# Attention of a decoder layer: the rows transposed by the host, key tiles added on GpSimd, and projections and sums moved between the scores

## The reference

```python
x = x + attn(layernorm(x))                       # 16 query heads, 4 key/value heads, 32 wide
#   Q = rmsnorm(xn @ Wq); V = xn @ Wv; K = rmsnorm(V)      (K is made from V)
#   p = softmax(Q K^T)       (the mask is empty: all 256 x 256 scores count)
#   y = rmsnorm((p V) @ Wo)
x = x + xattn(ctx, ctx, layernorm(x))            # long convolution, by Toeplitz matrices
x = x + ffn(layernorm(x))                        # ternary weights, int8 activations, 2048 wide
```

## Time and profile before

| | us |
|---|---|
| median of the three runs | 678.32 |
| profiled execution, device time | 679.29 |
| profiled execution, span of the core | 677.5 |
| TensorE busy | 613.7 |
| VectorE busy | 485.3 |
| ScalarE busy | 455.3 |
| GpSimd busy | 269.8 |

### The profile page before, as it was taken

The page is one execution under the profiler, slowest core; times in us unless marked ns, Lnnn a source line. Parts: engine busy times, 40 slices in busy tenths (PEclk is TensorE's granted clock), DMA queues, the critical chain, the costliest instruction groups (busy, mean ns, idle before and its releaser), DMA issues.

```text
span 677.5 us, 10465 instructions
## 1 busy us (share of the span) xinstructions
PE 613.7 (91%) x2818; PEld 342.0 (50%) x2818; DVE 485.3 (72%) x949; ACT 455.3 (67%) x799; POOL 269.8 (40%) x248
## 2 busy tenths in 40 slices
PE   5889999999999999989999999957799999899975
PEld 4525454535454543367777777743344444444432
DVE  3455767575758372437778877898999999999961
ACT  2363666666666667158988888864778778688771
POOL 1000000100010001137777777742566666666671
PEclk9959999999999997989999999987999999999997
DMA  8473144536261717026555656431042342432424
GB/s 312 126 207 85 40 105 145 122 126 138 110 176 71 208 41 178 24 79 193 169 169 171 192 170 174 156 110 44 16 109 63 82 105 62 106 79 62 94 48 108
DMA packets 75589, 80.89 MB, mean 119 GB/s; under 512 B 38000, under 2 KB 49776, under 8 KB 75440
## 3 DMA queue, kind: packets, MB, share of 16 engines
q1 hardware_dynamic: 75568, 80.65, 43.1%
HBM read 47.51 MB, written 4.28 MB: 76 GB/s over the span
## 4 chain that ended last, share of the span: by engine, by line
PE 26%; DVE 16%; issue 7%; POOL 3%; ACT 2%; DVEq 1%; DMA 1%; ACTq 0%; POOLq 0%; SPq 0%
PE ps L708 20%; DVE toep L1189 3%; PE ps L1069 3%; PE ps L1057 2%; DVE mb L1193 2%; POOL big L1306 2%; DVE ps L1175 1%; DVE ps L1156 1%; DVE mx L1160 1%; DVE qo L761 1%; POOL r L1302 1%; ACT asq L1104 1%; DMA act8t<-ys 1%; ACT kv L1093 1%; DVE x_all L1138 1%
## 5 line engine op out<-in xcount | busy, mean ns | idle before, releaser
L708 PE MATMUL ps<-kv,toep 128*128 128x288 f32 x640 | 157.3, 409 | 1.1 <-PEq L1368 1.1
L708 PEld LDWEIGHTS ps<-kv,toep 128*128 128x128 f32 x640 | 122.3, 192 | 36.1 <-issue 2.4
L1069 PE MATMUL ps<-wt,xqt 128*128 128x512 bf16 x512 | 123.4, 387 | 17.3 <-DVE toep L1189 16.5
L1306 POOL TENSOR_TENSOR big<-toep,wst 128x512 f32<-128x512 f32 x64 | 82.9, 1295 | 41.9 <-DVE toep L1189 41.9
L396 ACT ACTIVATE big<-ps,kscale 128x512 f32<-128x512 f32 x128 | 85.5, 696 | 12.7 <-PE ps L246 10.3
L1069 PEld LDWEIGHTS ps<-wt,xqt 128*128 128x128 bf16 x512 | 48.5, 99 | 79.1 <-DVE toep L1189 24.2
L246 PE MATMUL ps<-qx,kx 128*128 128x512 f32 x128 | 78.3, 633 | 10.5 <-ACT big L396 8.6
L761 DVE TENSOR_REDUCE qo<-big 128x2048 f32 (+1 forms) x32 | 72.2, 2258 | 0.0
L1057 PE MATMUL ps<-wt,act8t 128*128 128x512 bf16 x256 | 60.3, 390 | 7.9 <-DMA act8t<-ys 7.0
L696 POOL TENSOR_TENSOR kv<-ctx 128x768 f32<-128x768 f32 (+1 forms) x32 | 52.7, 1648 | 36.7 <-PE ps L708 27.9
L750 DVE TENSOR_TENSOR big<-ps,qd 128x1024 f32<-128x1024 f32 x32 | 39.2, 1224 | 37.1 <-ACT ys L840 34.6
(11 more groups left out here) (118 smaller groups left out, 958.9 us busy)
## 6 DMA issues: line engine op xcount, KB each, us to landing
qx<-kv SPq DMA_DIRECT2D x128, 128.0 KB, 2.4
wst<-in_wall SPq DMA_DIRECT2D x12, 1024.0 KB, 6.4
wst<-in_wall SPq DMA_DIRECT2D x48, 256.0 KB, 3.7
toep<-krows SPq DMA_DIRECT2D x32, 256.0 KB, 3.7
ctx<-in_ctxt SPq DMA_DIRECT2D x32, 192.0 KB, 2.6
out_y<-ot SPq DMA_DIRECT2D x16, 256.0 KB, 2.9
conv_part<-qo SPq DMA_DIRECT2D x14, 256.0 KB, 2.7
x_all<-in_x SPq DMA_DIRECT2D x2, 1536.0 KB, 14.5
```

The source lines that it names most:

```text
L708: mm = pe.matmul(m.ps[:, LB * r + lb, :].rearrange("p (b s) -> p b s", s=WIDE)[:, :, 0:PAIRS], m.toep[r][:, d * P:(d + 1) * P], m.kv[r][:, ...
L1069: mm = pe.matmul(bank[:, n % 2, :], xqt[r][:, k, :], wt[:, k, n * C:(n + 1) * C], start=(k == 0), stop=(k == CK - 1))
L1306: nc.gpsimd.tensor_tensor(act_w[r][:, n * C:(n + 1) * C], a[n % 2][:], gb[:, n * C:(n + 1) * C], ALU.mult).then_inc(s_w.sem, 1)
```

## The change

- The host also hands over x transposed (`xt`). Sync loads a row's 512 KB into a buffer (`xt_first`, `xt_s`: two parts of `qo`), one row ahead (`next_rows`), and the transposes, their copies and the normalisation ahead of them go. In their place the weights Wq and Wv are centred over their input channels once in the prologue (`column_sums`, `centre`), the inverse deviation cancels in the queries and keys (`ev1` enters the root), and the values are scaled by it on GpSimd (`values`).
- The order of scores becomes: all groups for the first half gp of the queries, then all for the second.
- GpSimd adds the two key tiles of the weights (`add_weights`), and `sum_weights` runs over the sums: 16 instructions a turn. Each half of `sum_weights` and `sum_values` has a place of its own among the last scores or behind them, and each half its own PSUM bank.
- v and q of row 1 move, but for half of q, from the prologue into turn 0.
- VectorE: residual of row i - 1 at the head of turn i; one sum of squares per position tile; the first reciprocal ahead of the second sum of squares, the norms and the queries' normalisation; the small tiles of the norms, but for `rqk`, lie in PSUM.
- ScalarE: the weight-magnitude sums behind the copies of queries and keys. Sync: the loads of the FFN's weights wait for the 7th score.

```diff
+    pts = sb("pts", [P, 6, C])
...
+    norms = TB[:, 1, :].rearrange("p (a t n) -> p a t n", t=TT, n=P // 2)
+    ssq, ve2, gr, nt = (norms[:, a, :, 0:NH] for a in range(4))
+    value_bank, weight_bank = (OB[:, 0, :], SB[:, 1, :]), (OB[:, 1, :], SB[:, 0, :])
...
     def score(n):
-        return n // 4, n // 2 % 2, n % 2
+        return n // 2 % HKV, n % 2, n // (2 * HKV)
...
+        def next_rows(i):
+            wait(sp, s_q, i, 2)
+            sp.dma_start(xt_s, xt[bass.ds(i + 1, 1)].rearrange("o p k t -> (o p) k t")).then_inc(d_xt.sem, 16)
...
-        sp.dma_start(x_all[:, 0], x_in[:, 0]).then_inc(d_x0.sem, 16)
         sp.dma_start(wv_s[:], wv.rearrange("(k p) n -> p k n", p=P)).then_inc(d_wv.sem, 16)
         sp.dma_start(wq_s[:], wq.rearrange("(k p) n -> p k n", p=P)).then_inc(d_wq.sem, 16)
+        sp.dma_start(xt_first, xt[0]).then_inc(d_xt0.sem, 16)
+        sp.dma_start(x_all[:, 0], x_in[:, 0]).then_inc(d_x0.sem, 16)
+        sp.dma_start(xt_s, xt[1]).then_inc(d_xt.sem, 16)
         sp.dma_start(x_all[:, 1], x_in[:, 1]).then_inc(d_x1.sem, 16)
...
+        next_rows(1)
         spread_q(1)
         with sp.Fori(2, B - 1) as i:
+            next_rows(i)
             spread_q(i)
+            wait(sp, s_sc, i, 7)
+            apart(sp)
...
         def qk_transpose(i, after=True):
...
             wait(pe, s_klo, i, 1)
+            q_rows(0)
+            wait(pe, s_qn, i, 2)
             for kv in range(HKV):
...
+            q_rows(1)
...
         def scores(i, n):
             kv, s, gp = score(n)
-            if n % 4 == 0:
+            if n < 2 * HKV and s == 0:
                 wait(pe, d_qx[kv], i, 4 * 16)
-            if n % 8 == 0:
-                wait(pe, s_kx, i, n // 8 + 1)
+            if n in (0, HKV):
+                wait(pe, s_kx, i, kv // 2 + 1)
             if n >= 2:
                 wait(pe, s_e, i, n - 1)
...
+        def sum_weights(i, gp, has_prev):
+            wait(pe, s_ps, i, HKV * (gp + 1))
+            if gp == 0 and has_prev:
+                wait(pe, s_x1, i - 1, 2)
+            for kv in range(HKV):
+                mm = pe.matmul(weight_bank[gp][kv * DH:(kv + 1) * DH, :], m.ones[:, 0:DH], pts[:, (gp * HKV + kv) % 6, :],
+                               start=True, stop=True)
+            mm.then_inc(s_den.sem, 1)
+
+        def sum_values(i, gp, s, has_prev):
+            if s == 0:
+                wait(pe, s_e, i, 2 * HKV * (gp + 1))
+            if s == 0 and gp == 0:
+                wait(pe, s_vo, i, 1)
+                if has_prev:
+                    wait(pe, s_x1, i - 1, 1)
+                else:
+                    wait(pe, s_qn, i + 1, 1)
+            for kv in range(HKV):
+                mm = pe.matmul(value_bank[gp][kv * DH:(kv + 1) * DH, :], vo[:, s, kv * DH:(kv + 1) * DH],
+                               pt[:, s, kv, gp * C:(gp + 1) * C], start=(s == 0), stop=(s == TT - 1))
+            if s == TT - 1:
                 mm.then_inc(s_pv.sem, 1)
         def project(i, first):
...
         def turn(i, has_prev=True, has_next=True):
-            makes_next = has_prev and has_next
             scores(i, 0)
             scores(i, 1)
             for t in range(TT):
-                if makes_next:
-                    x_transpose(i + 1, t)
+                if has_next:
+                    v(i + 1, t)
                 scores(i, 2 + t)
-            for t in range(TT):
-                if makes_next:
-                    v(i + 1, t)
-                scores(i, 4 + t)
             for n in range(TT * CK):
-                if makes_next:
+                if has_next and has_prev:
                     q(i + 1, n // CK, n % CK)
-                scores(i, 6 + n)
-            for t in range(TT):
-                scores(i, 14 + t)
-            sum_weights(i)
-            for t in range(TT):
-                if has_prev:
-                    q2_transpose(i - 1, t, has_next)
-            if not has_prev:
-                wait(pe, s_qn, i + 1, 2)
-            sum_values(i)
+                elif has_next and n < CK:
+                    q(i + 1, 1, n)
+                scores(i, 4 + n)
+                if n == 6:
+                    sum_weights(i, 0, has_prev)
+            scores(i, 12)
+            sum_values(i, 0, 0, has_prev)
+            scores(i, 13)
+            sum_values(i, 0, 1, has_prev)
+            scores(i, 14)
+            if has_prev:
+                q2_transpose(i - 1, 0, has_next)
+            scores(i, 15)
+            for s in range(TT):
+                sum_values(i, 1, s, has_prev)
+            sum_weights(i, 1, has_prev)
+            if has_prev:
+                q2_transpose(i - 1, 1, has_next)
...
+        pe.wait_ge(c_ones.sem, 1)
+        pe.wait_ge(d_wv.sem, 16)
+        column_sums(SB[:, 1, 0:P], wv_s, c_wvsum)
+        pe.wait_ge(c_wqadd.sem, 2)
+        column_sums(SB[:, 0, :], qn[:, 0:1, :], c_wqsum)
+        pe.wait_ge(d_xt0.sem, 16)
+        pe.wait_ge(c_wv.sem, 1)
+        for t in range(TT):
+            v(0, t, rows=xt_first)
+        for n in range(TT * CK):
+            if n < CK:
+                pe.wait_ge(c_wq.sem, n + 1)
+            q(0, n // CK, n % CK, rows=xt_first)
+
+        pe.wait_ge(d_xt.sem, 16)
+        for k in range(CK):
+            q(1, 0, k, bank=OB[:, 0, :])
...
+            for n in range(3):
+                exponential(i, n)
...
+                k_square(i + 1)
+            exponential(i, 3)
+            if has_next:
+                k_high(i + 1)
             exponential(i, 4)
+            if has_next:
+                v_copy(i + 1)
+            for n in range(5, 8):
                 exponential(i, n)
+            if has_next:
+                q_square(i + 1, 0 if has_prev else 1)
+            for n in range(8, 11):
                 exponential(i, n)
+            if has_next and has_prev:
                 q_square(i + 1, 1)
+            for n in range(11, 16):
                 exponential(i, n)
             for t in range(TT):
                 if has_prev:
                     q2_out(i - 1, t)
             if has_next:
-                if has_prev:
-                    weight_sums(i)
                 qk_out(i + 1)
+            if has_next and has_prev:
+                weight_sums(i)
             project(i, has_prev)
...
+        def rows_var(i, first=False):
+            if not first:
+                wait(dve, s_rs1, i - 1, 1)
             layer_norm_stats(i, stats, mv, ve1, s_bn1, s_mv1, s_ve1)
-            wait(dve, s_rs1, i, 1)
-            for t in range(TT):
-                if not first:
-                    wait(dve, s_xt, i - 1, t + 1)
-                nc.vector.tensor_scalar(xn[:, t, :], row(i, t), mv[:, t, 0:1], rs1[:, t:t + 1],
-                                        ALU.subtract, ALU.mult).then_inc(s_xn.sem, 1)
+            nc.vector.tensor_scalar(ev1[:], mv[:, :, 1], LN_EPS, RMS_EPS, ALU.add, ALU.mult).then_inc(s_ev1.sem, 1)
...
+        def qk_sums(i, t):
+            wait(dve, s_sq, i, t + 2)
+            nc.vector.tensor_reduce(ssq[:, t, :], sq[:, t, :].rearrange("p (n d) -> p n d", d=DH),
+                                    AX.X, ALU.add).then_inc(s_ssq.sem, 1)
+
         def qk_norms(i):
-            for part, (lo, hi) in enumerate(((0, NV + HQ), (NV + HQ, NH))):
-                wait(dve, s_sq, i, part + 2)
-                nc.vector.tensor_reduce(ssq[:, lo:hi], sq[:, lo * DH:hi * DH].rearrange("p (n d) -> p n d", d=DH),
-                                        AX.X, ALU.add).then_inc(s_ssq.sem, 1)
             wait(dve, s_ssq, i, 2)
-            nc.vector.tensor_scalar(ve2[:], ssq[:], 1.0 / DH, RMS_EPS, ALU.mult, ALU.add).then_inc(s_ve2.sem, 1)
+            wait(dve, s_ev1, i, 1)
+            nc.vector.scalar_tensor_tensor(ve2, ssq, 1.0 / DH, spread(ev1[:], NH), ALU.mult, ALU.add
+                                           ).then_inc(s_ve2.sem, 1)
...
+                nc.vector.tensor_tensor(gr, ve2, rqk[:], ALU.mult).then_inc(s_nr.sem, 1)
                 wait(dve, s_nr, i, 3 * k + 3)
-                nc.vector.scalar_tensor_tensor(nt[:], nt[:], -0.5, ve2[:], ALU.mult, ALU.mult).then_inc(s_nr.sem, 1)
+                nc.vector.scalar_tensor_tensor(nt, gr, -0.5, rqk[:], ALU.mult, ALU.mult).then_inc(s_nr.sem, 1)
                 wait(dve, s_nr, i, 3 * k + 4)
-                nc.vector.scalar_tensor_tensor(rqk[:], nt[:], 1.5, rqk[:], ALU.add, ALU.mult).then_inc(s_nr.sem, 1)
...
-        def turn(i, has_prev=True, has_next=True, rows=True):
+        def turn(i, has_prev=True, has_next=True, more=True):
+            if has_prev:
+                residual(i - 1)
             if has_next:
                 k_low(i + 1)
-                if rows:
-                    rows_in(i + 2)
+            if has_prev:
+                residual_norm(i - 1)
+            if has_next:
+                qk_sums(i + 1, 0)
+                if has_prev:
+                    invert_sums(i, 0)
+                qk_sums(i + 1, 1)
                 qk_norms(i + 1)
-                if not has_prev:
```

(50 more changed lines are left out.)

213 lines of the change are left out of this document (89 added, 124 removed).

## The result

| | before | after |
|---|---|---|
| median | 677.89 us (677.22 to 679.43, 6 runs) | 681.46 us (680.27 to 682.32, 6 runs) |
| ratio | | 1.0050, 95% interval 1.0035 to 1.0065 |
| profiled execution, device / span | 679.29 / 677.5 | 680.27 / 678.4 |
| TensorE / VectorE / ScalarE / GpSimd busy | 613.7 / 485.3 / 455.3 / 269.8 | 590.8 / 492.1 / 449.4 / 355.8 |

The change takes 22.9 us of work off TensorE and the kernel becomes 0.5% slower. Forecast: 680.0.

What follows compares the result with a forecast made beforehand. Bound: the loop of VectorE's chain and the query-spreading DMAs, not TensorE. Prologue 3.7, turn 0 1.7, six turns -3.3 and last turn -0.4 sum to +1.7 on 678.3: 680.0 us; 8-in-10 range 671.5 to 687.

Steps and rivals of the forecast that it cites:

- The loop: Attention turns: VectorE's chain and the query-spreading DMAs close each turn; 4.2 us won in front, 3.6 given back behind.
- A steady turn: Six middle attention turns: 31.7 us each after the change, 0.55 us won per turn, 3.3 us in six.
- The query waits: Start of a turn: query groups 1, 2, 3 land at 2.5, 5.1, 7.6; the new wait costs 1.6 us.
- The PSUM norms: Norm steps on VectorE with tiles in PSUM: no difference taken, 0.23 a step; bounds -6 to +6 us in all.
- Rival 1: Norm chain cheap in PSUM, 0.15 us a step: six turns give 6 more, sum 672.8 to 675; chance 0.30.
- fixed PSUM cost: Norm steps, by the skill page: some 0.065 us dearer each, 0.8 a turn, about 5 us more; not booked.
- Prologue: Before the first score: first score at 37.3 instead of 33.56, 3.7 us later, bounds 1.5 to 6.
- Wq lands near 8.2: Prologue: the Wq load, with 0.5 MB less in front of it, lands near 8.2 instead of 10.1.
- the bound of 1.5: Prologue's low bound: only 1.5 us later if Wq lands at 6.5 and the first spread lacks its extra 1.2.
- Turn 0: First attention turn, taking over v and half the queries of row 1: 32.2 against 30.48, +1.7 us, bounds 0 and +4.
- the last turn: Last attention turn: 29.1 against 29.5, -0.4 us, bounds -3.3 and +2.
- The clock rival: Start of each turn: TensorE's clock falls, costing 4 us a turn hit; two or three hits, 688 to 692; chance 0.10.

Runs made afterwards that it cites:

- run 2: Changed kernel with VectorE's order of before (both sums of squares and the norms ahead of the first reciprocal): 691.43 us, ratio 1.0198 to the kernel before.
- run 7: Changed kernel without GpSimd's adds of key tiles; TensorE sums both tiles with 16 instructions a half, as before: 693.21 us, ratio 1.0222 to the kernel before.
- run 1: The changed kernel once more, no edit: 682.78 us, ratio 1.0062 to the kernel before.
- run 3: Changed kernel with TensorE's order within a turn altered, pieces of the query projection filling the waits for queries: 678.00 us, ratio 0.9989 to the kernel before.
- run 4: Changed kernel with half the bytes (64 KB, not 128) in each of the 16 DMAs spreading the queries: 677.92 us, ratio 0.9994 to the kernel before.
- run 6: Changed kernel with the norm chain's four small tiles in SBUF, nothing else changed: 698.77 us, ratio 1.0303 to the kernel before.
- run 10: On top of run 3, the first half's second value sum moved behind score 15: 672.35 us, ratio 0.9920 to the kernel before.
- run 12: On top of run 10, eight extra matmuls that nobody reads in the last turn: 671.22 us, ratio 0.9879 to the kernel before.
- run 5: Changed kernel with the 16 query-spreading DMAs shared between Sync's and GpSimd's queues: 690.32 us, ratio 1.0184 to the kernel before.
- run 8: On top of run 3, GpSimd adds three groups of four, first half's value sums behind scores 14 and 15, smaller moves: 675.41 us, ratio 0.9964 to the kernel before.
- run 9: Changed kernel with the edits of run 6 and run 7 together: 691.16 us, ratio 1.0199 to the kernel before.
- run 11: Changed kernel with eight extra matmuls that nobody reads, six before turn 0 and two in it: 680.79 us, ratio 1.0035 to the kernel before.

## Why the prediction was right, and where two of its terms were not

**The loop: right.** That work taken off TensorE pays only where it shortens VectorE's chain, and that the change gives back behind the first reciprocal most of what it wins in front, is what both traces show: 3.9 won, 3.7 given back. Runs 2 and 7 show both halves of it: undoing VectorE's order costs 1.5, undoing the adds 1.6 a turn. The rows transposed by the host and the order of the scores were not tested by themselves; that the transposes taken off TensorE gave nothing is read from the traces.

**A steady turn: mechanism right, size 0.4 off.** Forecast 13.3 + 14.03 + 4.4 = 31.7; measured 13.60 + 14.08 + 4.42 = 32.1. The sum booked 0.55 a turn, 3.3 in six; five turns gave 0.17 each. The sixth took 32.86: one of its issues lasted 1.51 instead of 0.59. In runs 1 to 4, 6, 10 and 12 that turn is longer too, in 5, 7, 8, 9 and 11 it isn't. The traces have a hint. In the kernel of before, the changed one and every run but 5, an issue of over 1.3 us at a turn's start always had one transfer of the queue q8 (kind: instruction, 0.02 MB) in the same 10 us: among them this sixth turn, those of the seven runs named, and turn 0 of runs 1 and 11. The issues of the sixth turn in 7, 8, 9 and 11 have none beside them. Whether it is the cause wasn't tested, and what sets its time is open. The 0.3 in front is the step from score 10 to the first reciprocal: the sums start at 12.47 (forecast 12.2) and take 1.06, not the 0.9 that a quarter of the earlier trace rows gave. The query waits came where they were put (scores 4 and 6 at 5.16 and 7.68; forecast 5.1 and 7.6), though the views name a DMA only before some of them: these two scores start right when their groups land.

**The PSUM norms: right for the step, and the reason was missed.** "No difference": a step is 0.24 from the next, 0.233 before. Rival 1 needed less than 0.19. But the choice was priced by PSUM against SBUF alone, and its worth lies in what stands beside it: with GpSimd adding in the same stretch, the chain with its tiles in SBUF costs 2.1 a turn more (run 6), and nothing more where GpSimd adds nothing (run 9). I had weighed the norms' place and GpSimd's adds each by itself.

By the Trainium skill ("SBUF — State Buffer", section "SBUF: two separate sides") VectorE and GpSimd share one port pair as an exclusive lock, taken for the whole instruction by whichever starts first, and a VectorE operation takes part if it runs in a two-port mode or, against a GpSimd operation that reads SBUF, if it has two SBUF inputs. Run 6 agrees for GpSimd's adds: steps with two SBUF operands waited up to 1.1 beside them, while in the changed kernel those with one PSUM operand took 0.20 to 0.21. It does not agree for the whole of every GpSimd instruction, as the two steps beside the power of two columns were not held. That rule spoke about this change more than the fixed PSUM cost that I weighed; of that cost, 0.065 a step by the page, the runs show 0.03 at most.

**Prologue: wrong, +3.7 against +0.8 (+0.5 in run 1).** Two steps. "Wq lands near 8.2": it landed 5.6 after its issue at 1.2, as VectorE's wait shows, so the load queue's head start was worth 3.3, not 1.9. And the first score came 4.4 after the low parts, as in every other turn, where the sum kept the 5.6 of before. The first is worth 1.4 and the second 1.2 of the 2.9 missed:

```profile
6.89 1.22 DVE L663 TENSOR_TENSOR qn<-wq_s 128x1024 f32<-128x1024 f32 x1 [5.72 <-DMA wq_s<-in_wq]
8.15 0.69 DVE L665 TENSOR_TENSOR qn<-qn 128x512 f32<-128x512 f32 x1
...
11.01 2.48 DVE L526 SCALAR_TENSOR_TENSOR wq_s<-ps,wq_s 128x512 f32<-128x512 f32 x4 [1.57 <-PE ps L223]
```

The additions (1.22 and 0.69) and the column sum (2.08) came as estimated. The reason given for the column sum and the value projection, a slow start of TensorE, is seen in the durations (2.08 for two instructions of 512 columns, which take 1.02 in a steady turn) and not in the granted clock, which the profile has at 1.00 from 4 to 24; why they take so long there is open. Both conditions were named with the bound of 1.5, and the value took the middle; +0.8 lies below even that bound.

**Turn 0 and the last turn.** +1.7 forecast, +1.64 measured; -0.4 forecast and -0.7 measured. That these came so near is partly luck: in run 1 they are +4.3 and +0.7, with more of the slow clock in both and a late group of queries in turn 0.

**The clock rival** did not come in the steady turns (1.00 throughout, with 2.1 us of query waits in each, and the same in every run), but the clock does fall in turn 0 and in the last turn, where projections between the scores are missing; run 12 puts matmuls in their place in the last turn, and there it stays at 1.00. The Trainium skill ("TensorE: Matmul & The Clock Gate", "HAM oscillation") tells of a loop in which each iteration waits longer for its DMA than it computes, and has the slow clock back each time. The longest wait here is 1.1 in a turn of 32, so the six turns at 1.00 do not speak against that page; it did not bear on them.

So the total was right because two misses cancelled: the prologue 2.9 better than forecast, the six turns 3.0 worse. The medians differ by more than the profiles do (3.6 against 1.0): the profile of before was 1.4 above its median, the one of after 1.2 below, and for the latter run 1 shows two of the places, turn 0 and the last turn.

## What to carry to other kernels

Find the chain that closes the loop and count what is moved behind its start as well as what is taken off in front; when an engine takes over work, look at which operands its neighbour reads in the same stretch. After a reordering, look for the waits that it creates and move independent work into them: here the change alone cost 3.6 us, and these moves on top of it (runs 3 and 10) gave some 9. What such moves would give in the kernel of before wasn't tried. Where an engine goes sparse at a loop's end, extra work that nobody reads can be cheaper than the slow clock: it took 2.3 us off the last turn (run 12), and in turn 0 it showed no gain (run 11).
